# One pass per step in a software-pipelined attention kernel: P1 and P2 of a step each in one run, the output chain in the next step's P2

## The chip, the cores and the metric

One NeuronCore of one Trainium2 chip. The metric is device time in microseconds of one execution, the median of the runs shown.

## The reference, cut to what matters

Sixteen sequences x (256 × 128). For each: a convolution over 5 time steps to 252 × 256, ReLU and batch normalisation give h; then attention with 16 heads of 16 and a causal relative bias on the layer-normed h; then a quantised feed-forward layer, whose scales are maxima over all sixteen sequences.

```python
h = relu(win @ W.T + b); h = gamma * (h - running_mean) * rsqrt(running_var + eps) + beta
n = layernorm(h); q, k, v = n @ Wq, n @ Wk, n @ Wv          # 16 heads
sim = q k^T * scale + bias;  sim[upper triangle] = -max
h = h + softmax(sim) v @ Wo + bo
h = h + ffn(layernorm(h))     # act_qdq: scale from max|x| over the whole tensor
```

## The kernel before, in words

The time is in two parts. The first, the attention part, works batch by batch (16 batches) and ends at about 493 us; the feed-forward part follows and the change doesn't touch it.

**The pipeline.** Step b (-3 to 16) works on several batches at once. A stage is a tuple (name, offset, part) and handles batch b + offset. Each of TensorE, VectorE and ScalarE issues its stages in an order written out by hand (`PE_ORDER`, `DVE_ORDER`, `ACT_ORDER`, L449 to L462); `step_order` (L491) drops those whose batch doesn't exist. Every engine is in order, and semaphores named after what was made tie them together (`mx_r`: maxima ready, `q_ps`: q in PSUM, and so on). Steps 2 to 11 are a hardware loop over two steps; the rest is unrolled. For step 15 there is an order of its own (`LAST`, L481 to L488).

**The stages of a batch**, in order of dependence:
- xT (TensorE transposes the input), xh and xl (ScalarE, VectorE split it in two f16 parts), conv in six parts (TensorE, 32 matmuls), relu (ScalarE), two multiplies and adds on GpSimd (L977, L980), stats (VectorE), a norm of four small operations on GpSimd (`pool_norm`, L961), xn (ScalarE), xnT (TensorE), xnh and xnl.
- q, k, v: two parts each, 6 matmuls a part. qh and kh (ScalarE, L943), ql and kl (VectorE, L847) write f16 parts, and SyncE copies them by six DMAs into the stacks q_st and k_st (L1017). `va` takes v (ScalarE, L948).
- P1, twelve pieces: TensorE makes scores of two or four heads (bias matmul L665, products L668) in one of four PSUM banks, and VectorE takes the row maxima from it (L816). Piece n can't be written before VectorE has read the piece four before it.
- mT (TensorE transposes the 16 × 252 maxima, L676), mneg (ScalarE negates them, L931), and one DMA puts them into row 65 of q_st (L1032). P2 needs that row.
- P2, twelve pieces: TensorE makes transposed scores less the maximum (L686), in the same four banks, VectorE adds the bias (L807), ScalarE takes the exponential (L892).
- PV in four parts (L697, L701), osb (ScalarE copies each, L906).
- The output chain: OT0 and OT1 (transposition of the product, L710), on 0 and on 1 (reciprocal L855, product L857), onT (L718), onh (ScalarE, L954), onl (VectorE, L863), wo in two parts (L565), h2 (VectorE, L868), stats2 (L832, L837), the second norm on GpSimd, xn2 (ScalarE), x2T (L739), x2 (ScalarE, L957), ax (VectorE, largest value, L873).

**Order before.** Within step b: P2 pieces 0 to 5 of batch b, P1 pieces 0 to 11 of batch b+1, P2 pieces 6 to 11 of batch b. k of b+1 is made at the start of the step, q of b+2 and mT of b+1 near its end, among the P2 pieces; the last PV of a batch falls into the next step. The output chain of batch b-1 goes from the end of the first P2 half, through P1, to the second P2 half.

**PSUM.** Banks 0 to 3 hold scores, 4 and 5 PV, 6 and 7 are two rings of small stages (`MISC`, L507). `misc_free` makes a stage wait until the reader of the stage before it in its ring is done.

**GpSimd and SyncE** have one queue each: `pool_step` (L973) does batch b+2's h, its norm and the residual term, then the second norm of b-1; `sp_step` (L998) issues the stack DMAs, the next input, the store of h, then the DMA of mneg.

Of the kernel before, what the change touches and what calls it, by code (L numbers as in the profile page):

```python
# [30 lines left out]
B, T, D = 16, 256, 128  # L31
CTX = 5
N = T - CTX + 1
TT = N // 2
# [37 lines left out]
def audio_tower(nc, x, cw, cb, gamma, beta, rmean, rvar, wq, wk, wv, wo, bo, rel, wg, wu, wd, hot, eyes, out):  # L72
    with ExitStack() as ctx:
# [37 lines left out]
        def wait(eng, name, count):  # L111

            if isinstance(count, int) and count <= 0:
                return
            eng.wait_ge(S[name], count)
# [329 lines left out]
        def pieces(kind, off, first, end):  # L445
            return [(kind, off, n) for n in range(first, end)]

        P2, P1 = pieces("P2", 0, 0, 12), pieces("P1", 1, 0, 12)
        PE_ORDER = [P2[0], ("k", 1, 0), ("k", 1, 1), P2[1], ("conv", 2, 0), ("PV", -1, 3), P2[2], P2[3],  # L449
                    ("conv", 2, 1), P2[4], ("conv", 2, 2), P2[5], ("OT0", -1, 0), ("conv", 2, 3), ("conv", 2, 4),  # L450
                    ("PV", 0, 0), P1[0], ("OT1", -1, 0), P1[1], ("conv", 2, 5), P1[2], P1[3],
                    ("onT", -1, 0), P1[4], ("v", 1, 0), P1[5], P1[6], ("wo", -1, 0), P1[7],
                    ("wo", -1, 1), P1[8], ("v", 1, 1), P1[9], P1[10], ("xT", 3, 0), P1[11], ("PV", 0, 1), ("xnT", 2, 0),
                    P2[6], P2[7], P2[8], ("mT", 1, 0), ("q", 2, 0), P2[9], ("x2T", -1, 0), P2[10], ("q", 2, 1),
                    P2[11], ("PV", 0, 2)]
        DVE_ORDER = [P2[0], P2[1], ("kl", 1), P2[2], P2[3], P2[4], P2[5], ("on", -1, 0), ("ax", -2), P1[0], ("on", -1, 1),
                     P1[1], P1[2], P1[3], P1[4], ("onl", -1), P1[5], P1[6],
                     ("stats", 2), P1[7], ("h2", -1), P1[8], P1[9], ("stats2", -1), P1[10], ("xl", 3), P1[11],
                     ("xnl", 2), P2[6], P2[7], P2[8], P2[9], P2[10], ("ql", 2), P2[11]]
        ACT_ORDER = [P2[0], ("kh", 1), P2[1], ("osb", -1, 3), P2[2], P2[3], P2[4], P2[5], ("osb", 0, 0),  # L460
                     ("relu", 2), ("onh", -1), ("xn", 2), ("va", 1), ("xh", 3), ("xnh", 2), ("osb", 0, 1), ("xn2", -1),
                     P2[6], ("mneg", 1), P2[7], P2[8], ("x2", -1), P2[9], ("qh", 2), P2[10], ("osb", 0, 2), P2[11]]  # L462


        FF_BANKS = len(ff_banks)
        FF_BANK = [0, 1, 2]
        FF_DVE = {(-2, ("stats", 2)): [("wlo", 0, 2)], (-1, P1[2]): [("wlo", 0, 3)],
                  (B - 1, ("stats2", -1)): [("ffabs", 0)], (B, ("on", -1, 1)): [("ffint", 0)],
                  (B, ("onl", -1)): [("ffval", 0), ("ffpow", 0)],
                  (B, ("stats2", -1)): [("ax", -2)] + [("fflo", 0, j) for j in range(FF_BANKS)] + [("ax", -1)]}  # L470
        FF_ACT = {(-2, ("relu", 2)): [("whi", 0, 2)],
                  (-1, ("kh", 1)): [("whi", 0, 3)] + [("flipT", 0, i) for i in range(4)],
                  (-1, ("relu", 2)): [("flipT", 0, i) for i in range(4, 8)],
                  (B, ("onh", -1)): [("ffhi", 0, j) for j in range(FF_BANKS)]}
        FF_PE = {(B, ("onT", -1, 0)): [("ffspread", 0, 0)],
                 (B, ("wo", -1, 1)): [("ffT", 0, j) for j in range(FF_BANKS)]}
        for i in range(8):
            FF_PE[-1, P1[i]] = [("flip", 0, i)]


        PE_LAST = P2[0:4] + [("PV", -1, 3)] + P2[4:6] + [("OT0", -1, 0), ("PV", 0, 0), P2[6], ("OT1", -1, 0), P2[7],  # L481
                  P2[8], ("onT", -1, 0), ("PV", 0, 1), P2[9], P2[10], P2[11], ("wo", -1, 0), ("wo", -1, 1),
                  ("PV", 0, 2), ("x2T", -1, 0)]
        DVE_LAST = P2[0:6] + [("on", -1, 0), P2[6], ("on", -1, 1), P2[7], P2[8], ("ax", -2), ("onl", -1)] + P2[9:12] + [
                    ("h2", -1), ("stats2", -1)]
        ACT_LAST = P2[0:2] + [("osb", -1, 3)] + P2[2:6] + [("osb", 0, 0)] + P2[6:9] + [("onh", -1), ("osb", 0, 1)
                    ] + P2[9:12] + [("osb", 0, 2), ("xn2", -1), ("x2", -1)]
        LAST = {"pe": PE_LAST, "dve": DVE_LAST, "act": ACT_LAST}  # L488
        ORDERS = {"pe": (PE_ORDER, FF_PE), "dve": (DVE_ORDER, FF_DVE), "act": (ACT_ORDER, FF_ACT)}

        def step_order(engine, b):  # L491


            order, extra = ORDERS[engine]
            if not isinstance(b, int):
                return order
            if b == B - 1:
                order = LAST[engine]
            todo = []
            for st in order:  # L500
                if runs(b, st[1]):
                    todo += [st] + extra.get((b, st), [])
            return todo

        MISC = [[("conv", "relu_r", 1, 1, 2), ("v", "va_r", 1, 1, 1), ("xnT", "xnl_r", 1, 1, 2),  # L507
# [4 lines left out]
        misc_at = {m[0]: (r, i) for r, ring in enumerate(MISC) for i, m in enumerate(ring)}  # L512
        misc_bank = {name: MB + r for name, (r, i) in misc_at.items()}
        PIECES = [st for st in PE_ORDER if st[0] in ("P1", "P2")]
        score_bank = {(kind, n): i % 4 for i, (kind, off, n) in enumerate(PIECES)}

# [1 line left out]

            return not isinstance(b, int) or 0 <= b + off < B

        def bank_of(stage, b):

            return MB if stage == "OT1" and isinstance(b, int) and b >= B - 1 else misc_bank[stage]

        def misc_free(pe, stage, b):

            if bank_of(stage, b) != misc_bank[stage]:
                wait(pe, "va_r", B)
                return wait(pe, "on_r", 2 * (b - 1))
            r, i = misc_at[stage]  # L530
            i -= 1
            for back in range(5):
                while i >= 0:
                    _, name, per, n, off = MISC[r][i]
                    if runs(b - back if isinstance(b, int) else b, off):
                        return wait(pe, name, per * (b - back + off) + n)
                    i -= 1
                i += len(MISC[r])

# [29 lines left out]
        def pe_step(pe, b, par):  # L569
            odd = 1 - par  # L570
            for st in step_order("pe", b):
                name, off = st[0], st[1]
                part = st[2] if len(st) > 2 else 0
                c = b + off
                if name in misc_at:
                    bank = ps[:, bank_of(name, b), :]
                if name == "ffT":
                    wait(pe, "wdq_w", 1)
                    wait(pe, "sb_r", 12 * B)
# [110 lines left out]
                elif name == "PV":  # L690
                    g, vc = part, va[odd if off else par]
                    wait(pe, "exp_r", 12 * c + 3 * (g + 1))
                    wait(pe, "va_r", c + 1)
                    wait(pe, "osb_r", 4 * c + g - 1)
                    p = pt[0:TT, g % 2]
                    for i in range(4):
                        nc.tensor.matmul(ps[32 * i:32 * i + 32, OB + g % 2, 0:N], vc[0:TT, 0, 4 * g + i, :],  # L697
# [82 lines left out]
        def dve_step(dve, b, par):  # L780
            for st in step_order("dve", b):
# [67 lines left out]
                        qks[:, col:col + 1], hi[:, :, 0:N], ALU.mult, ALU.subtract).then_inc(S[name + "_r"], 1)  # L849
                elif name == "on":  # L850
                    t = st[2]
                    src = ps[0:TT, bank_of(f"OT{t}", b), :].rearrange("p (h e) -> p h e", e=32)
                    wait(dve, "oT_ps", 2 * c + t + 1)
                    wait(dve, "onT_ps", c)
                    nc.vector.reciprocal(rc[0:TT, t], src[:, :, DH]).then_inc(S["rc_r"], 1)  # L855
# [115 lines left out]
            nc.gpsimd.tensor_tensor(o[0:TT], o[0:TT], r[0:TT], ALU.mult).then_inc(S[f"nb{sfx}_r"], 1)  # L971

        def pool_step(pool, b, par):  # L973
            if runs(b, 2):
                c = b + 2
                wait(pool, "relu_r", c + 1)
                nc.gpsimd.tensor_tensor(h[0:TT], h[0:TT], bc[0:TT, 1:2, :].broadcast_to([TT, 2, C]), ALU.mult  # L977
                                        ).then_inc(S["v1_r"], 1)
                wait(pool, "v1_r", c + 1)
                nc.gpsimd.tensor_tensor(h[0:TT], h[0:TT], bc[0:TT, 2:3, :].broadcast_to([TT, 2, C]), ALU.add  # L980
                                        ).then_inc(S["h_r"], 1)
            if runs(b, 2):
                pool_norm(pool, c, mv, ve, rstd, nb, "")
                wait(pool, "h_r", c + 1)
                hc = hall_of(c).rearrange("p (t c) -> p t c", t=2)
                nc.gpsimd.tensor_tensor(hc, h[0:TT], bc[0:TT, 3:4, :].broadcast_to([TT, 2, C]), ALU.add
                                        ).then_inc(S["hb_r"], 1)
            if runs(b, -1):
                pool_norm(pool, b - 1, mv2, ve2, rstd2, nb2, "2")


        def load_x(sp, c):
# [4 lines left out]

        def sp_step(sp, b, par):  # L998
            odd = 1 - par
            if isinstance(b, int) and b == B - 1:  # L1000
                wait(sp, "p1_ps", 12 * B)
                wait(sp, "conv_ps", B)
                sp.dma_start(ff_view(0), ff_dram[0]).then_inc(S["ff_in0"], 16)
# [16 lines left out]
            if runs(b, -1):  # L1020
# [5 lines left out]
                else:  # L1026
                    sp.dma_start(res.ap()[bass.ds(c, 1)].rearrange("a p n -> (a p) n"),
                                 hall[0:TT, bass.ds(c, 1), :].rearrange("p a n -> p (a n)")).then_inc(S["spilled"], 16)
            if runs(b, 1):
                c = b + 1  # L1030
                wait(sp, "mneg_r", c + 1)
                sp.dma_start(qS[odd][P1_ROWS:P2_ROWS], mneg[:]).then_inc(S["mneg_in"], 16)  # L1032

        INIT = 2 + 2 + 4 + 1 + 1 + 2

# [554 lines left out]
```

## Time and profile before

| | us |
|---|---|
| median of 3 runs | 801.94 (795.84 to 803.84) |
| the profiled execution's own time | 800.07 |
| its span, first to last instruction | 798.1 |
| busy TensorE / VectorE / ScalarE / GpSimd | 620.4 / 603.7 / 452.2 / 134.3 |

Busy times are of the whole span, so an average over two unlike parts. TensorE matmuls overlap: in a group of rows, the time from one start to the next is what one takes of the engine, and the duration is longer than that. A row of the stretch view has the stretch, its length, each engine's busy time with its count of instructions, the granted TensorE clock (1.00 is 2.4 GHz, 0.50 is 1.2 GHz), the share and rate of DMA.

### The profile page before, as it was taken

To read this page: it belongs to the slowest core of one execution; us is meant where nothing else is said; L and a number is where in the kernel's file an instruction comes from. 1 tells how busy PE (TensorE), PEld (TensorE's weight loads), DVE (VectorE), ACT (ScalarE), POOL (GpSimd) and SP (SyncE) were. 2 spreads that over 40 slices of the span, in tenths; PEclk is the share of its full clock that TensorE was granted. 3 is DMA by queue.
4 is the path that set the end of the run, shared out by engine and by line. 5 is a ranking of instruction groups with operands and counts; after the bars stand their busy time and mean duration, and the time that the engine had idled before them with its cause. 6 is when DMAs were issued, how large, how long until landed. Compare 5 with 4: busy or idle time off the path is not lost. (4 is left out here: it accounts for less than half of the span.)

```text
span 798.1 us, 14680 instructions
## 1 busy us (share of the span) xinstructions
PE 620.4 (78%) x5169; PEld 466.2 (58%) x5169; DVE 603.7 (76%) x967; ACT 452.2 (57%) x647; POOL 134.3 (17%) x211
## 2 busy tenths in 40 slices
PE   4577989899998989898997975989999800006998
PEld 3446777777777777777775743434444300004997
DVE  7425888788888888898888767687479998994442
ACT  1424544665456654664466353436389966967772
POOL 4211232113311332123311000000024320000000
PEclk9789999999999999999999775999999955555999
DMA  7323213231333123331323102000134144400533
GB/s 201 114 29 48 42 21 60 49 60 27 46 46 59 36 37 51 54 53 20 61 41 54 54 14 83 9 1 1 68 140 182 58 175 155 130 0 1 149 116 100
DMA packets 39204, 52.82 MB, mean 66 GB/s; under 512 B 5724, under 2 KB 31772, under 8 KB 39164
## 3 DMA queue, kind: packets, MB, share of 16 engines
q1 hardware_dynamic: 38012, 51.49, 26.0%
q10 hardware_dynamic: 1152, 0.79, 0.4%
q8 instruction: 26, 0.43, 0.2%
q14 instruction: 14, 0.11, 0.1%
HBM read 22.74 MB, written 16.81 MB: 50 GB/s over the span
## 5 line engine op out<-in xcount | busy, mean ns | idle before, releaser
L816 DVE TENSOR_REDUCE mx<-ps 126x2 f32<-126x504 f32 (+1 forms) x192 | 125.6, 676 | 52.4 <-PE ps L668 50.9
L892 ACT ACTIVATE pt<-sbr 126x504 f32<-126x504 f32 x192 | 114.9, 617 | 26.0 <-DVE sbr L807 24.8
L807 DVE TENSOR_TENSOR sbr<-ps,biasT 126x504 f32<-126x504 f32 x192 | 120.0, 675 | 7.7 <-PE ps L686 7.2
L665 PE MATMUL ps<-biasN,antib 126*126 126x504 bf16 x192 | 74.9, 390 | 26.8 <-DMA k_st<-kl 26.8
L668 PE MATMUL ps<-k_st,q_st 65*126 65x252 f16 (+1 forms) x512 | 75.2, 249 | 0.0
L1159 PE MATMUL ps<-x2t,wgT 128*128 128x504 f16 x288 | 67.2, 394 | 8.1 <-ACT gat L1450 4.7
L1436 PE MATMUL ps<-wdT,raws 128*126 128x256 f16 x480 | 67.6, 283 | 4.5 <-DVE raws L1377 4.5
L668 PEld LDWEIGHTS ps<-k_st,q_st 65*126 65x126 f16 x512 | 60.6, 140 | 17.9 <-issue 3.4
L1135 PE MATMUL ps<-identf,sc 128*128 128x128 f32 x5 | 2.2, 434 | 86.7 <-DVE sc L1367 56.5
L686 PE MATMUL ps<-q_st,k_st 66*126 66x252 f16 (+1 forms) x512 | 68.4, 254 | 0.6 <-DMA q_st<-mneg 0.6
L977 POOL TENSOR_TENSOR h<-h,bc 126x512 f32<-126x512 f32 x16 | 20.4, 1277 | 269.4 <-ACT h L915 269.4
L1159 PE MATMUL ps<-x2t,wuT 128*128 128x504 f16 x288 | 63.0, 376 | 2.3 <-ACT raws L1464 2.3
L611 PE MATMUL ps<-wcT,xh 128*126 128x256 f16 x320 | 62.1, 279 | 0.0
L1436 PEld LDWEIGHTS ps<-wdT,raws 128*126 128x126 f16 x480 | 57.4, 142 | 6.8 <-DVE raws L1377 6.8
L926 ACT ACTIVATE xn<-h,nb,rstd 126x256 f32<-126x256 f32 x32 | 17.5, 593 | 70.2 <-POOL nb L971 70.2
L686 PEld LDWEIGHTS ps<-q_st,k_st 66*126 66x126 f16 x512 | 51.0, 140 | 8.8 <-issue 6.4
L1159 PEld LDWEIGHTS ps<-x2t,wgT 128*128 128x128 f16 x288 | 29.0, 102 | 43.4 <-DVE x2t L1265 8.8
L1135 PEld LDWEIGHTS ps<-identf,sc 128*128 128x128 f32 x5 | 0.9, 171 | 88.2 <-DVE sc L1367 56.8
L906 ACT ACTIVATE osb<-ps 128x252 f32<-128x252 f32 x64 | 23.7, 370 | 49.2 <-PE ps L710 45.5
L1530 POOL TENSOR_SCALAR sq<-sig 128x1512 int32<-128x1512 f32 x16 | 26.4, 1650 | 140.7 <-ACT sig L1489 123.4
L1159 PEld LDWEIGHTS ps<-x2t,wuT 128*128 128x128 f16 x288 | 27.6, 98 | 37.0 <-ACT raws L1464 5.9
L665 PEld LDWEIGHTS ps<-biasN,antib 126*126 126x126 bf16 x192 | 26.5, 138 | 32.7 <-DMA k_st<-kl 25.9
(189 smaller groups left out, 1471.3 us busy)
## 6 DMA issues: line engine op xcount, KB each, us to landing
up_raw<-raws SPq DMA_DIRECT2D x11, 756.0 KB, 3.2
x2t<-up_raw SPq DMA_DIRECT2D x6, 756.0 KB, 6.6
q_st<-qh SPq DMA_DIRECT2D x32, 128.0 KB, 4.0
k_st<-kh SPq DMA_DIRECT2D x32, 128.0 KB, 4.0
res<-hall SPq DMA_DIRECT2D x16, 252.0 KB
x2t<-res SPq DMA_DIRECT2D x16, 252.0 KB
out<-x2t SPq DMA_DIRECT2D x16, 252.0 KB
raws<-up_raw SPq DMA_DIRECT2D x5, 756.0 KB, 4.1
```

The source lines that it names most:

```text
L611: last = nc.tensor.matmul(bank[0:TT, t * C:(t + 1) * C], *products[i], start=(i == 0), stop=False)
L665: nc.tensor.matmul(dst, antib[0:TT], biasN[0:TT, heads[0]:heads[-1] + 1, N - w:N], start=True, stop=True)
L668: last = nc.tensor.matmul(dst[:, n * w:(n + 1) * w], qS[odd][0:P1_ROWS, hd, qt], kS[odd][0:P1_ROWS, hd, 0:w], start=False, stop=True, skip ...
L686: last = nc.tensor.matmul(ps[0:TT, score_bank[name, part], n * w:(n + 1) * w], kS[par][0:P2_ROWS, hd, kt], qS[par][0:P2_ROWS, hd, N - w:N] ...
L807: nc.vector.tensor_tensor(sbr[0:TT, n % 4].rearrange("p (h w) -> p h w", w=w), ps[0:TT, score_bank[name, n], 0:2 * N].rearrange("p (h w) - ...
L816: nc.vector.tensor_reduce(mx[0:TT, 0 if w == TT else 1, heads[0]:heads[-1] + 1], ps[0:TT, score_bank[name, n], 0:2 * N].rearrange("p (h w) ...
L892: nc.scalar.activation(pt[0:TT, n // 3 % 2, n % 3], sbr[0:TT, n % 4], ACT.Exp).then_inc(S["exp_r"], 1)
L906: nc.scalar.activation(osb[:, g], ps[:, OB + g % 2, 0:N], ACT.Copy).then_inc(S["osb_r"], 1)
L977: nc.gpsimd.tensor_tensor(h[0:TT], h[0:TT], bc[0:TT, 1:2, :].broadcast_to([TT, 2, C]), ALU.mult).then_inc(S["v1_r"], 1)
L1159: last = nc.tensor.matmul(ps[:, 3 * half + j, 0:2 * N], w[:, wp, k, m], xq[:, at:at + 2 * N], start=(i == 0), stop=(i == 5))
L1436: last = nc.tensor.matmul(ps[0:TT, s, t * C:(t + 1) * C], o[par][:, m, rows], wdT[:, w, m], start=(m == 0 and i == 0), stop=(m == MT - 1 a ...
L1530: nc.gpsimd.tensor_scalar(sq[t % 2][:], sig[t % 2][:], 65536.0, 0.0, ALU.mult, ALU.add).then_inc(S["sq_r"], 1)
```

## The change

The orders of the three engines are rewritten. A step starts with mT, OT0, OT1, q and k; then come all twelve pieces of P2 with the output chain of b-1 up to wo and the conv of b+2 between them; then all twelve of P1 with v, x2T, xT and xnT. q moves from offset 2 to offset 1, mT from 1 to 0, all of PV to offset 0. The special order for step 15 goes. The rings are redrawn, OT1 takes the PV bank 5. GpSimd does the second norm first in its step, and SyncE the DMA of mneg. Three side jobs of the feed-forward weights hang on other stages, and one `ax` that was done twice is done once.

```diff
-        PE_ORDER = [P2[0], ("k", 1, 0), ("k", 1, 1), P2[1], ("conv", 2, 0), ("PV", -1, 3), P2[2], P2[3],
...
+        PE_ORDER = [("mT", 0, 0), ("OT0", -1, 0), ("OT1", -1, 0), ("q", 1, 0), ("q", 1, 1), ("k", 1, 0), ("k", 1, 1)
+                    ] + P2[0:3] + [("onT", -1, 0), P2[3], ("conv", 2, 0), P2[4], ("conv", 2, 1), ("wo", -1, 0),
+                    ("wo", -1, 1), P2[5], ("conv", 2, 2), P2[6], ("PV", 0, 0),
+                    ("conv", 2, 3), P2[7], ("conv", 2, 4), P2[8], ("conv", 2, 5), P2[9], ("PV", 0, 1), P2[10], P2[11],
+                    ("v", 1, 0), P1[0], ("v", 1, 1), P1[1], ("PV", 0, 2), P1[2], ("x2T", -1, 0), P1[3], ("xT", 3, 0),
+                    P1[4], ("PV", 0, 3)] + P1[5:11] + [("xnT", 2, 0), P1[11]]
+        DVE_ORDER = [("on", -1, 0), ("on", -1, 1), ("ql", 1), ("kl", 1), ("ax", -2)] + P2[0:3] + [("onl", -1)
+                     ] + P2[3:7] + [("h2", -1)] + P2[7:9] + [("stats2", -1)] + P2[9:12] + P1[0:4] + [
+                     ("stats", 2), P1[4], P1[5], ("xl", 3)] + P1[6:12] + [("xnl", 2)]
+        ACT_ORDER = [("mneg", 0), ("qh", 1), ("kh", 1)] + P2[0:3] + [("onh", -1)] + P2[3:7] + [
+                     ("osb", 0, 0)] + P2[7:10] + [("relu", 2)] + P2[10:12] + [
+                     ("osb", 0, 1), ("xn2", -1), ("va", 1), ("osb", 0, 2), ("x2", -1), ("xh", 3), ("osb", 0, 3),
+                     ("xn", 2), ("xnh", 2)]
...
+        MISC = [[("q", "ql_r", 1, 1, 1), ("conv", "relu_r", 1, 1, 2), ("xnT", "xnl_r", 1, 1, 2)],
+                [("mT", "mneg_r", 1, 1, 0), ("OT0", "on_r", 2, 1, -1), ("k", "kl_r", 1, 1, 1), ("onT", "onl_r", 1, 1, -1),
+                 ("wo", "h2_r", 1, 1, -1), ("v", "va_r", 1, 1, 1), ("x2T", "x2_r", 1, 1, -1), ("xT", "xl_r", 1, 1, 3)]]
+        misc_bank["OT1"] = OB + 1
...
@@ PV in pe_step
+                    if g == 1:
+                        wait(pe, "on_r", 2 * c)
@@ pool_step
+            if runs(b, -1):
+                pool_norm(pool, b - 1, mv2, ve2, rstd2, nb2, "2")
             if runs(b, 2):
...
-            if runs(b, -1):
-                pool_norm(pool, b - 1, mv2, ve2, rstd2, nb2, "2")
@@ sp_step
+            if runs(b, 0):
+                unregistered(sp, b)
+                wait(sp, "mneg_r", b + 1)
+                sp.dma_start(qS[par][P1_ROWS:P2_ROWS], mneg[:]).then_inc(S["mneg_in"], 16)
...
-            if runs(b, 1):
-                c = b + 1
-                wait(sp, "mneg_r", c + 1)
-                sp.dma_start(qS[odd][P1_ROWS:P2_ROWS], mneg[:]).then_inc(S["mneg_in"], 16)
```

## Rows read from the trace of the kernel before

**Rows 1.** The page: busy time of each engine, its share of the span, instructions.
```profile
PE 620.4 (78%) x5169; PEld 466.2 (58%) x5169; DVE 603.7 (76%) x967; ACT 452.2 (57%) x647; POOL 134.3 (17%) x211
```
**Rows 2.** Stretches: twelve steps, a later step (14), the tail of the part.
```profile
89.98:400.89 310.91, 285.52 (x2949) 238.01 (x2947) 261.90 (x517) 176.36 (x349) 73.63 (x132) 1.00 0.28 46
426.25:453.87 27.62, 22.45 (x203) 17.58 (x202) 21.07 (x40) 12.20 (x26) 1.18 (x4) 0.88 0.23 40
453.87:477.97 24.10, 18.28 (x167) 12.51 (x167) 15.93 (x31) 14.79 (x30) 1.18 (x4) 0.73 0.14 45
```
**Rows 3.** Waits of VectorE in those twelve steps: total, times, longest.
```profile
DVE mx L816 <- PE ps L668: 24.7, 12, 3.0
DVE ql L847 <- ACT qh L943: 11.6, 12, 1.0
```
**Rows 4.** In order of time, one step: mT, q, mneg, the next transposition.
```profile
321.43 0.60 PE L676 MATMUL ps<-identf,mx 126*16 126x126 f32 x4 [0.38 <-DVE mx L816]
322.11 0.38 PE L640 MATMUL ps<-xnh,wqT 128*128 128x252 f16 x2
322.33 0.38 PE L640 MATMUL ps<-xnl,wqT 128*128 128x252 f16 x2
323.12 0.35 ACT L931 ACTIVATE mneg<-ps 16x252 f16<-16x252 f32 x1
323.62 0.62 PE L739 MATMUL ps<-identf,xn 126*128 126x126 f32 x4 [0.47 <-ACT mneg L931]
```
**Rows 5.** The page's DMA issues: KB each, median us from issue to landing.
```profile
q_st<-mneg SPq DMA_DIRECT2D x16, 8.0 KB, 1.8
```
**Rows 6.** VectorE in order of time: start, duration.
```profile
332.56 0.25 DVE L855 RECIPROCAL rc<-ps 126x16 f32<-126x16 f32 x1
332.84 0.42 DVE L857 TENSOR_TENSOR on<-ps,rc 126x256 f32<-126x256 f32 x1
333.18 0.67 DVE L873 TENSOR_REDUCE amax_x<-x2t  x1
```
**Rows 7.** VectorE and ScalarE: q's low part, run of P2, exponentials.
```profile
326.17 0.74 DVE L847 SCALAR_TENSOR_TENSOR ql<-ps,qks,qh 128x504 f16<-128x504 f32 x1 [0.99 <-ACT qh L943]
326.83 1.98 DVE L807 TENSOR_TENSOR sbr<-ps,biasT 126x504 f32<-126x504 f32 x3
325.39 0.66 ACT L943 ACTIVATE qh<-ps,qks 128x504 f16<-128x504 f32 x1
312.63 0.59 ACT L954 ACTIVATE onh<-ps 128x504 f16<-128x504 f32 x1 [0.49 <-PE ps L718]
304.97 2.39 ACT L892 ACTIVATE pt<-sbr 126x504 f32<-126x504 f32 x4 [0.62 <-DVE sbr L807]
```
**Rows 8.** TensorE in order of time, starts: OT0, conv, P1 pieces, PV, xnT, P2 pieces.
```profile
305.57 0.60 PE L710 MATMUL ps<-identf,osb 128*126 128x128 f32 x4
306.01 0.27 PE L611 MATMUL ps<-wcT,xh 128*126 128x256 f16 x1
...
317.35 0.38 PE L665 MATMUL ps<-biasN,antib 126*126 126x504 bf16 x1
317.78 0.38 PE L665 MATMUL ps<-biasN,antib 126*126 126x504 bf16 x1
318.97 0.63 PE L697 MATMUL ps<-pt,va 126*32 126x252 f32 x8
319.75 0.65 PE L624 MATMUL ps<-identf,xn 126*128 126x126 f32 x4
320.23 0.82 PE L686 MATMUL ps<-q_st,k_st 66*126 66x252 f16 x8
```
**Rows 9.** TensorE at the start of P1 in step 14, and two stretches of step 15.
```profile
438.31 0.68 PE L665 MATMUL ps<-biasN,antib 126*126 126x504 bf16 x1 [3.03 <-DMA k_st<-kl]
452.00:456.00 4.00, 2.64 (x21) 2.04 (x23) 2.86 (x6) 3.64 (x8) 0.24 (x2) 0.83 0.02 4
456.00:462.00 6.00, 6.00 (x52) 4.03 (x52) 3.97 (x8) 4.24 (x9) 0.00 (x0) 0.50 0.43 132
```

More of the change, by code:

```diff
@@ L448, in audio_tower @@
         P2, P1 = pieces("P2", 0, 0, 12), pieces("P1", 1, 0, 12)
-        PE_ORDER = [P2[0], ("k", 1, 0), ("k", 1, 1), P2[1], ("conv", 2, 0), ("PV", -1, 3), P2[2], P2[3],
[L450 to L462, printed above, removed]
+        PE_ORDER = [("mT", 0, 0), ("OT0", -1, 0), ("OT1", -1, 0), ("q", 1, 0), ("q", 1, 1), ("k", 1, 0), ("k", 1, 1)
[4 more added lines that the diff above has]
+                    P1[4], ("PV", 0, 3)] + P1[5:11] + [("xnT", 2, 0), P1[11]]
@@ L467, in audio_tower @@
         FF_DVE = {(-2, ("stats", 2)): [("wlo", 0, 2)], (-1, P1[2]): [("wlo", 0, 3)],
[L468 to L473, printed above, removed]
+                  (B - 1, P2[11]): [("ffabs", 0)], (B, ("on", -1, 1)): [("ffint", 0)],
+                  (B, ("onl", -1)): [("ffval", 0), ("ffpow", 0)], (B, ("ax", -2)): [],
+                  (B, ("stats2", -1)): [("fflo", 0, j) for j in range(FF_BANKS)] + [("ax", -1)]}
+        FF_ACT = {(-2, ("relu", 2)): [("whi", 0, 2)], (-1, ("relu", 2)): [("whi", 0, 3)],
+                  (-1, ("va", 1)): [("flipT", 0, i) for i in range(4)],
+                  (-1, ("xh", 3)): [("flipT", 0, i) for i in range(4, 8)],
                   (B, ("onh", -1)): [("ffhi", 0, j) for j in range(FF_BANKS)]}
@@ L478, in audio_tower @@
             FF_PE[-1, P1[i]] = [("flip", 0, i)]
[L481 to L488, printed above, removed]
         ORDERS = {"pe": (PE_ORDER, FF_PE), "dve": (DVE_ORDER, FF_DVE), "act": (ACT_ORDER, FF_ACT)}
@@ L496, in step_order @@
                 return order
-            if b == B - 1:
-                order = LAST[engine]
             todo = []
@@ L503, in step_order @@
             return todo
-        MISC = [[("conv", "relu_r", 1, 1, 2), ("v", "va_r", 1, 1, 1), ("xnT", "xnl_r", 1, 1, 2),
[4 rows of a table removed]
+        MISC = [[("q", "ql_r", 1, 1, 1), ("conv", "relu_r", 1, 1, 2), ("xnT", "xnl_r", 1, 1, 2)],
+                [("mT", "mneg_r", 1, 1, 0), ("OT0", "on_r", 2, 1, -1), ("k", "kl_r", 1, 1, 1), ("onT", "onl_r", 1, 1, -1),
+                 ("wo", "h2_r", 1, 1, -1), ("v", "va_r", 1, 1, 1), ("x2T", "x2_r", 1, 1, -1), ("xT", "xl_r", 1, 1, 3)]]
         misc_at = {m[0]: (r, i) for r, ring in enumerate(MISC) for i, m in enumerate(ring)}
         misc_bank = {name: MB + r for name, (r, i) in misc_at.items()}
+        misc_bank["OT1"] = OB + 1
         PIECES = [st for st in PE_ORDER if st[0] in ("P1", "P2")]
@@ L519, in runs @@
             return not isinstance(b, int) or 0 <= b + off < B
-        def bank_of(stage, b):
-            return MB if stage == "OT1" and isinstance(b, int) and b >= B - 1 else misc_bank[stage]
         def misc_free(pe, stage, b):
-            if bank_of(stage, b) != misc_bank[stage]:
-                wait(pe, "va_r", B)
-                return wait(pe, "on_r", 2 * (b - 1))
+            if stage not in misc_at:
+                return
             r, i = misc_at[stage]
@@ L574, in pe_step @@
                 c = b + off
-                if name in misc_at:
-                    bank = ps[:, bank_of(name, b), :]
+                if name in misc_bank:
+                    bank = ps[:, misc_bank[name], :]
                 if name == "ffT":
@@ L851, in dve_step @@
                     t = st[2]
-                    src = ps[0:TT, bank_of(f"OT{t}", b), :].rearrange("p (h e) -> p h e", e=32)
+                    src = misc(f"OT{t}")[0:TT].rearrange("p (h e) -> p h e", e=32)
                     wait(dve, "oT_ps", 2 * c + t + 1)
```

4 rows, old and new, of the table MISC are left out of this document.

## The prediction

> **What bounds the kernel now.** I read the page first: TensorE 78% and VectorE 76% of the span [rows 1], so no engine is plainly the bound. That is a mean over two unlike parts, so the next view is the stretches. In the twelve steps from 89.98 to 400.89 us (310.91 us, 25.9 a step) VectorE is busy 261.9 us, 21.8 a step, and TensorE 285.5, 23.8 a step, both at clock 1.00 [rows 2]. Of each step VectorE is free for only 4.1 us. The waits say where: 2.1 us a step before the first maximum of P1, 1.0 before ql [rows 3], and 1.0 in smaller ones. So the step is VectorE's work plus the waits that the order leaves in it, and TensorE has only 2.1 us of slack. The question for the change is one sum: how long does VectorE wait per step in the new order?
>
> **What goes.** The first wait of [rows 3], for the stacks of k, which were written just ahead of P1. In the new order k is stacked at the start of the step, with all of P2 (over 10 us) before P1. With P2's tail no longer spread around ql and kl, the old waits there are replaced by those below. At most 4.1 us a step are to be gained.
>
> **What comes: the seam.** mT needs all twelve maxima, and P2 needs mneg. Before, P2 pieces 6 to 11 of the older batch stood between; now nothing of P2 or P1 can run there. I walk it, with T = 0 where VectorE ends the last maximum. Intervals on an engine are start to start: VectorE takes 0.66 for ql and (1.98 - 0.68)/2, rounded down with the other long runs to 0.6, for a P piece [rows 7]; an "on" takes 0.28 + 0.34 [rows 6]; TensorE takes 0.11 for a matmul of q, k, v, wo or conv [rows 4, 8], 0.44 for a transposition group, 0.43 for a P1 piece, 0.78 for a PV, and (0.82 - 0.17)/3 = 0.22 for a P2 piece [rows 8]; a result is there some 0.17 after the next start.
> - mT starts at 0.06 and is done at 0.66 (0.60 [rows 4]); mneg (0.35) ends at 1.04. OT0 shares mT's bank, so it waits for mneg: 1.19 (0.15 later, as 323.12 + 0.35 to 323.62 [rows 4]), done 1.79. VectorE has done xnl by 0.5 and waits 1.3 us for it. OT1 is done by 2.2, on 0 and on 1 by 3.1.
> - q can start at 2.07 and takes 12 × 0.11 = 1.31, so 3.5; qh 0.66 [rows 7], so ql starts at 4.2: 1.1 us of waiting. k ends at 4.85, kh at 5.5, kl at 5.6: 0.7 us. Then kl and ax take 1.3, and VectorE takes the first P2 piece at 6.8.
> - The DMA of mneg (1.8 us to landing [rows 5]) is down at 2.9, behind q and k, and costs nothing. On SyncE it stands first, before the six stack DMAs, which wait for qh anyway.
>
> Seam: 3.1 us of waiting.
>
> **The chain inside P2.** onl waits for onh, which ScalarE issues after the exponentials of pieces 0 to 2. VectorE ends piece 2 at 8.7, its exponential takes 0.62, onh 0.59 [rows 7]: onl starts at 9.9, where VectorE was free at 8.6: 1.3 us. wo follows onl and holds TensorE 1.3 us; behind it P2 piece 5 is ready at 12.4, VectorE was free at 11.7: 0.7 us. From there each P2 piece has a conv part (0.55 to 0.66) or a PV ahead of it on TensorE against 0.6 on VectorE: another 0.9 us over pieces 6 to 8. P2 ends at 19.1.
>
> **P1.** Pieces 1 to 5 have v (0.66), PV 2, x2T, xT and PV 3 between them: TensorE needs 1.1 us for v and a piece, 1.2 for a PV and a piece, against 0.6. x2T moreover waits for ScalarE, which does osb 1, xn2 and va in that order after the last exponential, and va frees the bank: 1.1 us for TensorE. VectorE waits 0.1 + 0.5 + 0.8 + 1.4 + 0.3 = 3.1 us here. Pieces 6 to 11 have nothing between and it doesn't wait. TensorE is ahead at the end: piece 11 is written after piece 7 is read, so TensorE is idle for about 1.8 us up to mT.
>
> **The sum.** Waits 3.1 + 1.3 + 0.7 + 0.9 + 3.1 = 9.1; with the work of 21.8 a step takes 30.9, against 25.9: +5.0. The walk's unlike parts may be off by half a microsecond each; from both sides I put the step at 29.5 to 32 (below, where ScalarE takes onh without the full 1.3; above, 0.2 us of TensorE issue time before each PV). Steps 1 to 13 are such steps: +65. Step 14 has no conv; it took 27.6 before, in part at half clock [rows 2], and comes to about the same. The tail from mneg of batch 15 to its first OT0 took 24.1 [rows 2]; here P2 comes with nothing but the chain of batch 14, about 20.6: -3.5. GpSimd's second norm goes ahead of h: its input is ready at 17.3, relu only at 19.2, so neither waits. The moved weight jobs and the saved duplicate ax lie beside other work: 0. Together 800.1 + 61.5 = 861.6, if the clock stays up. The profiled execution is 1.9 us under the median, so 863.5 as a median.
>
> **The clock.** It has two levels, 1.2 and 2.4 GHz. In the twelve steps it stays at 1.00 with TensorE idle 2.1 us a step. It fell in step 14 after 3.03 us without a matmul (the next one takes 0.68 [rows 9] for 0.38 [rows 8]), and again when, around mneg of batch 15, TensorE was busy 2.64 of 4 us; the following 6 us run at 0.50 [rows 9]. In the new seam TensorE has, in 4 us, mT, OT0 and OT1 and nothing else: about 1.5 us of matmuls. That is less than at the second fall and more than at the first. I therefore take falls in two of three seams of steps 1 to 14, 9 of 14. A fall there doubles OT1, q and k, on whose ends ql and kl hang: 0.44 + 2.62 = 3.1, and 0.3 for onT behind them: 3.4 us. Bounds for one: 0, where it falls to low and is back before q; 6.5, half of the 13 us at the low level in the 24.1 us at mean clock 0.73 [rows 2]. 9 × 3.4 = 31, so **894 us**.
>
> The Trainium skill, page "TensorE: Matmul & The Clock Gate", section "HAM oscillation — how this bites in real kernels", says that a kernel whose waits recur in every tile falls back in every tile and pays the return each time. By it all 14 seams would fall. The trace of before shows two falls near such waits, and none in the twelve regular steps.
>
> **Rivals.**
> - *Clock stays up.* For: the seam's longest single gap, 1.8 us, is shorter than the 3.03 at the first fall [rows 9]. Against: the second fall. 864 us. Chance 0.20.
> - *Falls in every seam, or twice in a step* (the second where TensorE waits some 2 us for onl before wo). 14 × 3.4 = 48 gives 911; twice gives 95 and 959. Chance 0.22. The first of these is what the page's rule would do.
> - *Faster: the seam is covered.* One mechanism: between the last maximum and the first P2, VectorE has xnl, two on, ql, kl and ax, 3.8 us of work, about as long as the way mT, mneg, DMA, P2 (4 us), and TensorE's lead over VectorE feeds the rest. Then the 4.1 us of waiting go, and TensorE's 23.8 [rows 2] becomes the step: -2.1 × 12 = -25, 777 us. It decides where the new waits stay under 4.1 us a step in sum. Against: the fillers themselves hang on mneg, q and k in line, and the seam alone costs 3.1. Chance 0.06.
> - *No difference.* The new waits come out at just the old 4.1: 802 us. Chance 0.04.
>
> The forecast has the rest, 0.48, with its own range of 875 to 910. The range that should hold the time 8 times in 10 goes from 852 (clock up, step at 30) to 930 (all seams fall and some steps twice). A measurement tells about 1% from no change. Faster 0.06, within 1% 0.04, slower 0.90.
>
> **What would show it.** Right: mneg rows 30 to 35 us apart; VectorE waiting for OT0, qh, kh and onh in every step, 1.3, 1.1 (more at the low clock), 0.7 and 1.3 us; no wait for the k stack before P1; TensorE waiting for onl before wo and for ScalarE before x2T; matmuls of q and k at 0.42 a pair's step where the clock is low. Wrong: steps under 29 us; a first P2 piece that waits for the DMA of mneg; VectorE's waits in the P1 run under 1.5 us, or a clock of 1.00 through all steps, which is the first rival.

## The result, and the profile after

The changed kernel takes 863.21 us (861.31 to 878.71, 4 runs) against 799.49 (4 runs): ratio 1.079, interval 1.075 to 1.084, so 8% slower. The ratio and its interval are without the run of 878.71 us, whose mean granted clock was 0.885 where the other three have 0.903 to 0.909. Forecast were 894 us, with 875 to 910 as its own range, and 852 to 930 in all. The time lies in the wide range only: it came out at the first rival, the clock that stays up (864 us, chance 0.20). The profiled execution took 861.31 us; the sum of the prediction without its clock term was 861.6.

Stretches of the kernel after, cut at the starts of mneg: step 1, step 2, steps 3 to 12, step 14, and the tail.

```profile
89.31:119.39 30.08, 24.39 (x246) 19.82 (x246) 21.73 (x42) 15.33 (x30) 6.15 (x11) 1.00 0.30 41
119.39:151.83 32.44, 26.05 (x246) 20.99 (x246) 22.55 (x43) 15.24 (x29) 6.13 (x11) 0.95 0.27 38
151.83:459.09 307.26, 244.09 (x2460) 198.12 (x2460) 224.04 (x430) 152.55 (x290) 61.41 (x110) 1.00 0.28 39
488.62:517.85 29.23, 21.69 (x208) 17.01 (x208) 20.07 (x37) 12.81 (x25) 1.19 (x4) 0.94 0.25 37
517.85:538.11 20.26, 14.42 (x124) 10.54 (x124) 13.83 (x27) 10.49 (x20) 1.18 (x4) 0.71 0.19 53
```

Against [rows 2]: the ten steps take 30.7 us each where they took 25.9, with VectorE busy 22.4 (21.8 before) and TensorE 24.4 (23.8). The work is the same; VectorE now stands 8.3 us of a step instead of 4.1, and TensorE 6.3 instead of 2.1. The tail from mneg of batch 15 to its OT0, which starts at 538.68, fell from 24.1 to 20.8 us (the last row above is cut 0.6 us earlier).

The waits of both engines in the same ten steps (total, times, longest):

```profile
DVE mx L801 <- PE ps L651: 26.4, 40, 1.2
DVE rc L840 <- PE ps L695: 13.9, 10, 1.4
DVE ql L832 <- ACT qh L928: 12.7, 10, 1.3
DVE sbr L792 <- PE ps L669: 12.6, 30, 0.7
DVE onl L848 <- ACT onh L939: 11.7, 10, 1.2
DVE kl L832 <- ACT kh L928: 4.0, 10, 0.6
```
```profile
PE ps L548 <- DVE onl L848: 20.5, 10, 2.1
PE ps L659 <- DVE mx L801: 14.6, 10, 1.5
PE ps L703 <- DVE kl L832: 9.6, 10, 1.0
PE ps L724 <- ACT va L933: 8.0, 10, 0.9
PE ps L695 <- ACT mneg L916: 6.2, 10, 0.6
PE ps L578 <- ACT x2t L942: 4.2, 10, 0.4
```

The wait for the k stack that led [rows 3] is gone, as forecast. What has come is a row for every place that the walk named. One seam in order of time on VectorE, with the releasers of its waits:

```profile
304.82 0.67 DVE L826 TENSOR_TENSOR xnl<-ps,xnh 128x504 f16<-128x504 f32 x1
306.93 0.26 DVE L840 RECIPROCAL rc<-ps 126x16 f32<-126x16 f32 x1 [1.44 <-PE ps L695]
309.56 0.74 DVE L832 SCALAR_TENSOR_TENSOR ql<-ps,qks,qh 128x504 f16<-128x504 f32 x1 [1.29 <-ACT qh L928]
310.69 0.74 DVE L832 SCALAR_TENSOR_TENSOR kl<-ps,qks,kh 128x504 f16<-128x504 f32 x1 [0.38 <-ACT kh L928]
311.35 0.67 DVE L858 TENSOR_REDUCE amax_x<-x2t  x1
311.93 1.85 DVE L792 TENSOR_TENSOR sbr<-ps,biasT 126x504 f32<-126x504 f32 x3
```

The last maximum ends at 304.9. From there VectorE has nothing of P1 or P2 until 311.9, 7.0 us (walked: 6.8).

### The profile page after: what moved, and what is told of

It is laid out like the page before. It is cut to its first block and busy times, and to the rows that moved or that the text cites. A ratio compares the mean times of both kernels' runs of the same rounds, so it can differ in the third digit from the quotient of the medians.

```text
span 859.2 us, 14638 instructions
## 1 busy us (share of the span) xinstructions
PE 623.9 (73%) x5169; PEld 463.8 (54%) x5169; DVE 609.5 (71%) x966; ACT 459.9 (54%) x647; POOL 134.5 (16%) x211
## 5 line engine op out<-in xcount | busy, mean ns | idle before, releaser
L801 DVE TENSOR_REDUCE mx<-ps 126x2 f32<-126x504 f32 (+1 forms) x192 | 122.9, 677 | 51.0 <-PE ps L651 50.9
L792 DVE TENSOR_TENSOR sbr<-ps,biasT 126x504 f32<-126x504 f32 x192 | 122.7, 677 | 24.4 <-PE ps L669 23.1
L950 POOL TENSOR_TENSOR ve<-mv,epsc 126x2 f32<-126x2 f32 x32 | 6.2, 195 | 383.9 <-DVE mv L822 383.9
L669 PEld LDWEIGHTS ps<-q_st,k_st 66*126 66x126 f16 x512 | 53.0, 140 | 7.7 <-issue 3.7
L548 PE MATMUL ps<-woT,onh 128*126 128x256 f16 x128 | 27.5, 302 | 31.9 <-DVE onl L848 31.9
L1144 PEld LDWEIGHTS ps<-x2t,wuT 128*128 128x128 f16 x288 | 27.6, 98 | 36.9 <-ACT raws L1449 5.9
L594 PE MATMUL ps<-wcT,xl 128*126 128x256 f16 x160 | 44.2, 276 | 0.0
L594 PEld LDWEIGHTS ps<-wcT,xh 128*126 128x126 f16 x320 | 40.8, 138 | 2.7 <-issue 2.7
```

Source lines behind the costliest of these rows:

```text
L548: last = nc.tensor.matmul(out_ap, a, w, start=(i == 0), stop=(i == len(todo) - 1))
L594: last = nc.tensor.matmul(bank[0:TT, t * C:(t + 1) * C], *products[i], start=(i == 0), stop=False)
L669: last = nc.tensor.matmul(ps[0:TT, score_bank[name, part], n * w:(n + 1) * w], kS[par][0:P2_ROWS, hd, kt], qS[par][0:P2_ROWS, hd, N - w:N] ...
L792: nc.vector.tensor_tensor(sbr[0:TT, n % 4].rearrange("p (h w) -> p h w", w=w), ps[0:TT, score_bank[name, n], 0:2 * N].rearrange("p (h w) - ...
L801: nc.vector.tensor_reduce(mx[0:TT, 0 if w == TT else 1, heads[0]:heads[-1] + 1], ps[0:TT, score_bank[name, n], 0:2 * N].rearrange("p (h w) ...
L1144: last = nc.tensor.matmul(ps[:, 3 * half + j, 0:2 * N], w[:, wp, k, m], xq[:, at:at + 2 * N], start=(i == 0), stop=(i == 5))
```

## The experiments

All start from the changed kernel unless said. "A clean step" is a steady step, mneg to mneg, in which no matmul ran at 1.2 GHz; the changed kernel's is 30.8 us.

**The seam alone.**

```diff
-PE_ORDER = [("mT", 0, 0), ("OT0", -1, 0), ("OT1", -1, 0), ("q", 1, 0), ("q", 1, 1), ("k", 1, 0), ("k", 1, 1)
+PE_ORDER = [("OT0", -1, 0), ("mT", 0, 0), ("q", 1, 0), ("q", 1, 1), ("OT1", -1, 0), ("k", 1, 0), ("k", 1, 1)
-DVE_ORDER = [("on", -1, 0), ("on", -1, 1), ("ql", 1), ("kl", 1), ("ax", -2)] + P2[0:3]
+DVE_ORDER = [("on", -1, 0), ("ax", -2), ("on", -1, 1), ("ql", 1), P2[0], ("kl", 1)] + P2[1:3]
-("OT0", "on_r", 2, 1, -1)        # in MISC
+("OT1", "on_r", 2, 2, -1)
-misc_bank["OT1"] = OB + 1
+misc_bank["OT0"] = OB + 1
```

> The seam alone: OT0 goes to the PV bank and ahead of mT, OT1 to the ring bank behind q, and VectorE takes on 0, ax, on 1, ql, P2 piece 0, kl. Theory A (a step is VectorE's work of 21.8 us plus its waits, and these add up): the first P2 piece comes about 2 us earlier after the last maximum (7.0 us in the changed kernel, 5.0 here), the step goes from 30.8 to about 28.8, the kernel by -2.0 x 14 = -28 us, to 833 to 838. Theory B (TensorE's stream is the limit, VectorE's waits only show it): TensorE has the same matmuls, the wait moves into P2 and P1, and the kernel gains under 8 us.

846.48 us, -17, ratio to before 1.060 (1.055 to 1.065). The clean step is 29.7: -1.1, half of what I expected. The first P2 piece starts 5.3 us after the last maximum (296.87 to 302.13; expected 5.0), but kl now stands behind it instead of ahead of it. The trace names a wait that I had overlooked: k waits 0.8 us in each step for VectorE's on 1, because OT1 and k share a bank, and the first P2 piece comes late for it:

```profile
302.13 0.68 DVE L792 TENSOR_TENSOR sbr<-ps,biasT 126x504 f32<-126x504 f32 x1 [1.23 <-PE ps L669]
```

Neither theory had the number. A had the way; a part of the wait did move into P2, as B says.

**The P1 run alone.**

```diff
-("v", 1, 0), P1[0], ("v", 1, 1), P1[1], ("PV", 0, 2), P1[2], ("x2T", -1, 0), P1[3], ("xT", 3, 0),
-P1[4], ("PV", 0, 3)] + P1[5:11] + [("xnT", 2, 0), P1[11]]
+("v", 1, 0), P1[0], ("v", 1, 1), P1[1], P1[2], ("PV", 0, 2), P1[3], P1[4], ("x2T", -1, 0), P1[5],
+P1[6], ("xT", 3, 0), P1[7], ("PV", 0, 3), P1[8], P1[9], ("xnT", 2, 0), P1[10], P1[11]]
...
-("xh", 3), ("osb", 0, 3), ("xn", 2), ("xnh", 2)]        # ACT_ORDER
+("xn", 2), ("xh", 3), ("osb", 0, 3), ("xnh", 2)]
```

> The P1 run alone: PV 2, x2T, xT and PV 3 are spread to behind pieces 2, 4, 6 and 7, and ScalarE's xn goes ahead of xh and osb 3. Theory A: VectorE's waits in the P1 run fall from 2.7 to about 1 us a step, and TensorE's idle time before mT shrinks; -1.7 x 14 = -24 us, 836 to 843. Theory B: TensorE is bound there anyway, the waits come in front of other pieces, under 8 us of gain.

854.85 us, -8 only, ratio 1.068 (1.062 to 1.073). By steps it is clear: step 2 is clean and takes 29.01 us, -1.8 as A says. In each of steps 3 to 13 the granted clock falls, and steps 3 to 10 take 30.6 to 32.2. Neither theory has this: the gain is A's in the one clean full step, and near B's in the kernel. The first three full steps:

```profile
89.65:118.00 28.35, 24.00 (x246) 19.85 (x246) 21.57 (x42) 15.10 (x30) 6.15 (x11) 1.00 0.31 44
118.00:147.01 29.01, 24.22 (x246) 19.85 (x246) 22.34 (x43) 15.01 (x29) 6.15 (x11) 1.00 0.31 42
147.01:177.68 30.67, 25.79 (x246) 20.82 (x246) 22.37 (x43) 15.01 (x30) 6.15 (x11) 0.94 0.29 40
```

VectorE's busy time is the same in the last two; TensorE's is 1.6 us longer for the same 246 matmuls. The gain was made and given back to the clock. (With xT, VectorE's xl moves behind P1 piece 8.)

**The chain alone.**

```diff
-("kh", 1)] + P2[0:3] + [("onh", -1)] + P2[3:7]        # ACT_ORDER
+("kh", 1), P2[0], ("onh", -1)] + P2[1:7]
```

> The chain alone: ScalarE does onh behind the exponential of P2 piece 0, not of piece 2. Theory A: VectorE's wait of 1.17 us for onh goes to about 0.1, the following 0.73 before piece 5 stays: -1.05 x 15 = -16 us, 845 to 850. Theory B: under 5 us.

857.22 us, -6, ratio 1.072 (1.067 to 1.077). Again the step tells more than the time. Three starts of mneg:

```profile
241.79 0.37 ACT L916 ACTIVATE mneg<-ps 16x252 f16<-16x252 f32 x1 [2.04 <-PE ps L659]
273.14 0.37 ACT L916 ACTIVATE mneg<-ps 16x252 f16<-16x252 f32 x1 [1.97 <-PE ps L659]
302.82 0.37 ACT L916 ACTIVATE mneg<-ps 16x252 f16<-16x252 f32 x1 [2.04 <-PE ps L659]
```

31.35 us with a fall of the clock, 29.68 without: the clean step is 1.1 shorter, as expected, and one fall costs 1.67. Only three of steps 1 to 13 are clean, so the kernel has a third of the gain.

**The three together.** All the edits of the last three diffs in one kernel.

> The three together. Theory A, waits add up: -28 - 24 - 16 = -68, 795 us, about the time of the kernel before. Theory B, or one limit behind the others: TensorE needs 23.3 us of matmuls a step, so with steps near 26 part of the three gains overlaps and it stays above 810.

809.09 us, ratio to before 1.010 (1.005 to 1.015). The step is 27.07 at clock 1.00: -3.7, where the three clean gains give 1.1 + 1.8 + 1.1 = 4.0. The waits add up nearly; the kernel gains 54 us where its three parts alone gained 31, because here none of steps 1 to 13 has a fall, and two of the three parts had one in most steps. Theory A's 795 was 14 us too low: it still had 2.0 a step for the seam, which alone had given 1.1. Against the kernel before, 1% is no clear difference.

**A longer gap in the seam.** Three and seven spare activations between mT and mneg, in every step.

```diff
+for i in range(3):        # or 7
+    wait(act, "spent", 3 * c + i)
+    nc.scalar.activation(spare[:, 0:N], misc("mT")[0:H, 0:N], ACT.Copy, scale=-1.0).then_inc(S["spent"], 1)
 nc.scalar.activation(mneg[:, 0:N], misc("mT")[0:H, 0:N], ACT.Copy, scale=-1.0).then_inc(S["mneg_r"], 1)
```

> Three more small activations of ScalarE (into a spare tile) between mT and mneg, in each of 16 steps. The single gap of TensorE between mT and OT0 grows from 0.65 to about 1.9 us, and the way to the first P2 by 1.3. Theory C (the clock falls where TensorE has little to do over the whole seam): the clock falls in most steps and a step takes 30.8 + 1.3 + the price of a fall, 1.7 to 3.4, so 34 to 35.5. Theory D (what decides is one unbroken gap, and this one is still short): no falls, 32.1 a step, 881 us.

905.06 us. TensorE's gap is 1.8 us, +1.15. A step without a fall takes 31.92 (298.81 to 330.73), the mean of steps 2 to 10 is 33.9: falls in most steps, for some 2 us a step. That is what theory C says. But this is one execution, and an execution further down has falls in most steps without the longer gap; that the gap brought these isn't shown.

> Seven of them: the gap grows to about 3.6 us, longer than the 3.03 before the fall in step 14 of the kernel before. Both theories have the clock fall in every step. It gives the price of a fall: step time less 30.8 less 3.0. From the one fall in the changed kernel (32.44 less 30.78) it is 1.7; as I had predicted it, 3.4. 13 such steps: 861 + 47 + 24 = 932 by the first, 955 by the second.

957.5 us in one execution, near the 955 of the higher price; the gap is 3.4 us, +2.75, and from step 3 to 13 the clock is low twice in every step, around OT0, q and k and again at wo:

```profile
250.00:287.55 37.55, 28.43 (x248) 23.03 (x247) 22.42 (x44) 17.72 (x36) 6.15 (x11) 0.86 0.23 31
```

30.8 + 2.75 leaves 4.0 us for the low clock in this step. A mean clock of 0.86 between full and half speed is 10.5 us of the step at the low level (37.55 x 0.14 / 0.5). So the 4.0 us is not the price of one short fall but of two low stretches, the first of them longer.

**Less work for TensorE.** The conv without the products of its weights' low part.

```diff
-products += [(xh[:, rows], wcT[:, 0, i, :]), (xl[:, rows], wcT[:, 0, i, :]), (xh[:, rows], wcT[:, 1, i, :])]
+products += [(xh[:, rows], wcT[:, 0, i, :]), (xl[:, rows], wcT[:, 0, i, :])]
```

> The conv leaves out the products with the low part of its weights (10 of 32 matmuls, 1.1 us of TensorE a step; the result loses that part). Theory A: only the waits behind conv parts shrink, 0.3 us a step, and 858. Theory B, TensorE's stream is the limit: 1.1 us a step, 846 or less.

883.08 us (882.84 and 883.33), 20 us slower with a third of the conv left out. Both theories failed. Its stretch of ten steps:

```profile
117.51:446.74 329.23, 261.63 (x2360) 205.43 (x2360) 223.47 (x430) 151.73 (x290) 61.56 (x110) 0.90 0.26 36
```

32.9 us a step at clock 0.90. VectorE is busy as before; TensorE has 100 matmuls fewer in ten steps (2360 for 2460) and is yet busy longer than in the changed kernel (26.2 against 24.4 us a step). The shortest steps with one fall take 31.8 us, so a clean one would be 30.1, and step 1, clean in both kernels, takes 29.53 against 30.08. The work left out gained 0.6 and the clock cost 2.7. Why the clock falls here isn't shown: both runs have it, but the changed kernel itself took up to 878.71 us, and 888.86 in the next run.

**The same steps at another time.** Two or four spare activations in step 0 alone; all later steps do what they did. The activations were to make everything after them later.

```diff
+for i in range(2 if isinstance(c, int) and c == 0 else 0):        # or 4
+    wait(act, "spent", i)
+    nc.scalar.activation(spare[:, 0:N], misc("mT")[0:H, 0:N], ACT.Copy, scale=-1.0).then_inc(S["spent"], 1)
```

> The changed kernel with two spare activations between mT and mneg in step 0 alone: everything after comes some 0.9 us later, each step does the same as before. Theory E (whether the clock falls in a seam hangs on the time at which the seam comes, so a later start can bring falls into every step with the same work): mean clock 1.00 or falls in most of steps 2 to 12; a step with a fall takes 32.4, without 30.8. Theory F (the work in the seam alone decides): steps 2 to 12 stay at 30.8, 862.

888.86 us in one execution, 26 us more than the changed kernel.

```profile
286.05:422.51 136.46, 110.70 (x984) 89.27 (x984) 89.67 (x172) 60.97 (x116) 24.55 (x44) 0.90 0.25 35
```

Four steps of 34.1 us at clock 0.90, with VectorE busy 22.4 in each as always. Of steps 2 to 12, seven have two low stretches like these and two have none. The low stretches lie in two places. First q and the start of k (two matmuls of q took 0.22 start to start in [rows 4], here 0.42), then wo, behind its wait for onl:

```profile
286.56 1.15 PE L696 MATMUL ps<-identf,osb 128*126 128x128 f32 x8 [0.63 <-ACT mneg L921]
287.51 0.62 PE L624 MATMUL ps<-xnh,wqT 128*128 128x252 f16 x2
287.93 0.62 PE L624 MATMUL ps<-xnl,wqT 128*128 128x252 f16 x2
...
297.73 0.45 PE L549 MATMUL ps<-woT,onh 128*126 128x256 f16 x1 [2.05 <-DVE onl L849]
297.96 0.42 PE L549 MATMUL ps<-woT,onl 128*126 128x256 f16 x1
```

> The same with four, some 1.7 us later. Theory E: of this and the run with two at least one has falls in most steps, and then 863 + 1.7 x 10 = 880 us. Theory F: 863.

866.75 us in one execution. Steps 2 to 12 have no fall, and steps 2 to 10 take 30.8 each. Theory F fails: the same work in the seam has two falls a step in one execution and none in another.

Whether the delay did that is another question, and the traces say that it isn't shown. First ScalarE's spare activations (in the changed kernel, without them, mneg itself), then the first P2 piece; without, with two and with four of them:

```profile
64.94 0.37 ACT L916 ACTIVATE mneg<-ps 16x252 f16<-16x252 f32 x1 [1.23 <-PE ps L659]
69.66 1.09 PE L669 MATMUL ps<-q_st,k_st 66*126 66x252 f16 x10 [1.91 <-DMA q_st<-mneg]
```
```profile
64.78 0.77 ACT L919 ACTIVATE spare<-ps 16x252 f16<-16x252 f32 x2 [1.23 <-PE ps L660]
69.17 1.09 PE L670 MATMUL ps<-q_st,k_st 66*126 66x252 f16 x10 [1.58 <-DMA q_st<-mneg]
```
```profile
65.77 1.58 ACT L919 ACTIVATE spare<-ps 16x252 f16<-16x252 f32 x4 [1.23 <-PE ps L660]
70.93 1.09 PE L670 MATMUL ps<-q_st,k_st 66*126 66x252 f16 x10 [1.71 <-DMA q_st<-mneg]
```

Two activations put mneg 0.67 us later, four 1.48, not 0.9 and 1.7. The first P2 piece of step 0 waits for the DMA of mneg, and with two activations it starts 0.5 us earlier than without any; mneg of step 1 follows at 88.82 us where the changed kernel has 89.31. With four it starts 1.3 us later, and 0.8 of that was there before the first spare activation ran. The clock has its own times too: its last rise before these rows is at 51.7, 51.9 and 53.3 us. So the executions differ by as much as the delays, and the one with the many falls wasn't late at all. That a later start brings falls, as theory E has it, is not shown; what sets an execution with falls apart from one without stays open.

**All filler ahead of the waits.** The lessons in one order.

```diff
+PE_ORDER = [("OT0", -1, 0), ("OT1", -1, 0), ("mT", 0, 0), ("q", 1, 0), ("q", 1, 1), ("onT", -1, 0),
+            ("k", 1, 0), ("k", 1, 1)] + P2[0:3] + [("wo", -1, 0), P2[3], ("wo", -1, 1), ("conv", 2, 0), P2[4],
+            ("conv", 2, 1), P2[5], ("conv", 2, 2), P2[6], ("PV", 0, 0), P2[7], ("conv", 2, 3), P2[8],
+            ("conv", 2, 4), P2[9], ("conv", 2, 5), ("PV", 0, 1), P2[10], P2[11],
...
+DVE_ORDER = [("on", -1, 0), ("on", -1, 1), ("ax", -2), ("ql", 1), ("onl", -1), P2[0], ("kl", 1)] + P2[1:5] + [
+             ("h2", -1)] + P2[5:8] + [("stats2", -1)] + P2[8:12] + P1[0:4] + [
...
+ACT_ORDER = [("mneg", 0), ("qh", 1), ("onh", -1), ("kh", 1)] + P2[0:6] + [
...
+misc_bank.update(OT0=OB + 1, OT1=OB, onT=OB + 1)
+if g == 0: wait(pe, "on_r", 2 * c)        # PV
+if g == 1: wait(pe, "onl_r", c)
```

> All filler ahead of the wait: OT0, OT1 and onT in the PV banks, OT0 and OT1 before mT, onT and onh between q and k, wo behind the first P2 pieces, PV 0 before P2 piece 7, and the P1 run spread as in the earlier run. Theory A: VectorE waits 0.5 us in the seam, about 1 in P2 and 1 to 1.5 in P1, so a step takes 24.5 to 25.3 against 25.9 of the kernel before: 785 to 795. Theory B: TensorE's 23.3 us of matmuls with its own waits keep it at 26 or more, 802 or above.

779.89 us (777.85 to 781.13), ratio to the kernel before 0.978 (0.972 to 0.983): faster than both, by about 2% than the kernel before. Twelve steps and VectorE's waits in them and a bit more (13 steps):

```profile
88.84:393.48 304.64, 286.71 (x2952) 237.09 (x2952) 264.04 (x516) 182.04 (x348) 74.02 (x132) 1.00 0.34 47
```
```profile
DVE sbr L794 <- PE ps L669: 19.8, 40, 0.7
DVE mx L803 <- PE ps L651: 11.5, 25, 0.5
DVE ql L834 <- ACT qh L930: 9.2, 13, 1.1
```

25.4 us a step. The waits are 3.1 a step (expected 2.5 to 3), the seam's share 0.7. The step is only 0.5 us shorter than that of the kernel before, which is 6.3 us of the 20 between the two profiled executions. More comes from the end of the part, step 14 and the tail to OT0 of batch 15:

```profile
418.47:440.86 22.39, 20.12 (x208) 15.68 (x208) 20.46 (x40) 12.67 (x25) 1.20 (x4) 1.00 0.35 49
440.86:458.65 17.79, 11.96 (x117) 8.68 (x117) 13.16 (x25) 10.79 (x21) 1.19 (x4) 0.78 0.19 61
```

Together 40.2 us for 51.7 in [rows 2], with no fall in step 14.

**Is that luck of timing too?** The two spare activations, once, in the improved order and in the kernel before.

> The improved order with the same two spare activations in the first mT to mneg, which brought falls into nearly every step of the changed kernel (863 to 889 us). Theory G (a fall needs TensorE idle in the seam, and here it has OT0, OT1, q and k around mT): no falls whatever the time, 780 plus 1 us. Theory H (this order was lucky in its timing too): 1.7 us for each fall, 795 or more.

> The kernel before with the same two activations once. G: 796 to 803 as without them, clock 1.00 in steps 1 to 12. H: falls in several steps, 810 or more, and the comparison of the two kernels would hang on timing alone.

781.22 and 802.08 us. Their twelve steps, in that order:

```profile
91.09:395.71 304.62, 286.63 (x2952) 237.10 (x2952) 264.05 (x516) 181.88 (x348) 73.82 (x132) 1.00 0.34 47
```
```profile
91.86:402.59 310.73, 285.53 (x2949) 238.00 (x2946) 261.88 (x517) 176.38 (x349) 73.62 (x132) 1.00 0.28 46
```

304.62 for 304.64 us and 310.73 for 310.91, both at clock 1.00, though mneg of step 1 comes 2.3 us later in the one (91.09 for 88.84) and 1.9 in the other (91.86 for 89.98); 1.3 and 1.9 of that were there before the spare activations. So each order was traced at two timings and had no fall in these steps. The times alone say the same of more executions: the kernel before stayed within 795.5 to 803.8 us in all of its 22 runs, the improved order within 777.85 to 781.22 in five, while the changed kernel and its two delayed forms went from 861 to 889 in six. That favours theory G. That it is the work of TensorE around mT which keeps the clock up was not tested by itself.

## Why the prediction was right, and where it was not

**The bound and the sum: right.** That the step is VectorE's work plus its waits was the right frame; the three parts undone one by one each shortened the clean step, and together they added up to within 0.3 us a step. By places, walked and measured per step: for OT0 1.3 and 1.4; ql 1.1 and 1.3; kl 0.7 and 0.4; onl 1.3 and 1.2; the P2 pieces 0.7 + 0.9 and 1.3; P1 3.1 and 2.6. Listed waits 9.1 and 8.1, busy time 21.8 and 22.4, step 30.9 and 30.8. The busy time grew without more work: a step has 43 instructions of VectorE in both kernels, and their durations add up to 24.6 us in both, but they overlap less. So two errors of the walk, waits 1.0 too long and busy time 0.6 too short, partly cancel. The DMA of mneg is hidden in every steady step, as said (in step 0 it is not). The tail was 20.6 and is 20.8; step 14 was put at 27.6 and took 29.2. Sum 861.6, measured 861.3. That they agree to 0.3 us is in part luck: steps 1 to 13 took 63.0 us more than before and not 65, with a fall of 1.7 among them, and step 14 took 1.6 more and not the same. Nor did the 1.9 us that were added from the profiled execution to the median stand: with a fourth run the median before is 799.49, under the profiled 800.07.

**The P1 run: oversized by 0.5.** x2T waits 0.8 to 0.9 us for va, not 1.1, and its piece comes 1.2 us late, not 1.4.

**The clock: the step that failed.** I put falls in 9 of 14 seams at 3.4 us each. The profiled execution has one in the seams of steps 1 to 14 (step 2, 32.44 us); its fall in step 14 comes 10 us after mneg, and the kernel before has one there too. Two things were wrong in that step. The price: one fall costs 1.67 us (31.35 less 29.68), half of what I took, since it ends before k is done; in step 2 two matmuls of q start 0.42 apart from 121.56, and from 123.5 they are at 0.22 again. And the count: I read from a busy share whether a fall comes, as if like seams must behave alike. They don't: steps 2 to 12 ran with one fall (861.3 us), with two in most steps (888.9) and with none (866.8). What I had as the likeliest case and what I had as a rival are executions of one loop, and that the wide range held the time is no merit of the clock term. What decides between them stays open.

**The page's rule.** The Trainium skill, page "TensorE: Matmul & The Clock Gate", section "HAM oscillation — how this bites in real kernels", tells of a kernel that falls back in every tile, where the wait for a transfer is longer than the tile's matmuls. That is one long wait. I had carried it over to a step with several short ones: 1.5 us before mT, 0.65 behind it and 2.1 before wo. By the rule so stretched all 14 seams fall, 911 us with my price and 887 with the measured one. The run with the gap of 3.4 us has falls in every step, as the page says; the changed kernel's own seam had them in one execution and not in another.

**The rival on the other side**, a covered seam, was wrong for this order, since its fillers hung on mneg, q and k in line. It was right as a mechanism: with fillers that depend on nothing late, the seam's waits fall from 3.1 us to 0.7. The kernel with them beats the one before, though more through the end of the part than through the steps.

## What to carry to other kernels

When the only work that could cover a round trip is moved away from it, walk the seam with starts and ends from the trace: the filler that is left covers it only if it doesn't itself wait for the trip, and a shared PSUM bank can make it wait. Put the fillers that need nothing new ahead of the instruction that waits, and spread TensorE's side work evenly over a run whose consumer is slower. And judge an order by its steps at one clock before believing the kernel's time: here a wait saved of 1.1 or 1.8 us a step showed as about a third of that, and a loss showed where matmuls were left out. And before reading a delay's effect off a time, look in the trace whether anything came later.

## What the runs showed of the hardware that I had not expected

- The same work in steps 2 to 12 ran with one fall of the clock (861 us), with two in most steps (889) and with none (867), in three executions whose step 1 starts at 89.3, 88.8 and 90.6 us. The kernel before and the improved order, traced at two timings each, had none.
- With 10 of 32 conv matmuls a step left out, both runs took 20 us longer: clock 0.90, VectorE's waits for P1 4.0 us a step for 2.6 and for qh 2.1 for 1.3. That leaving them out brings the falls isn't shown.
- A fall in the seam costs 1.67 us where it stretches OT, q and a part of k; two falls in a step, the second at wo, 3.3 (34.1 less 30.8).
- In the four steps of 34.1 us no single wait of TensorE is longer than 2.1 us, and the clock still fell twice in each, the second time at the end of the 2.05 us before wo.
